# One layer of attention and routed low-rank feed-forward: low-rank products stacked into one fp32r product, the routing bias moved to GpSimd, the first norm moved whole to ScalarE, and a reordered prologue

## The reference, cut to what matters

```python
# x: (16, 256, 128) float32; two heads of 64
def layer(x):
    x = x + layernorm(attention(layernorm(x)))   # q, k, v, rotary on half of each head, softmax, Wo
    x = x + layernorm(ffn(layernorm(x)))
    return x

def ffn(x):                        # E = 4 experts of ranks 1, 2, 4, 8 (15 in all)
    base = x @ W.T
    proj = l2norm(x @ Wp.T + bp)   # 32 wide
    lw   = softmax(proj @ l2norm(sim) * exp(min(temp, CLAMP_MAX)))
    gate = where(arange(4) == argmax(lw), lw, 0)
    return base + sum_e gate[e] * (x @ Wd[e].T) @ Wu[e].T
```

## Time and profile before

| | |
|---|---|
| median of 3 executions | 150.28 us (150.28 to 150.42) |
| profiled execution | 150.36 us, of which the profiler's span is 148.6 us |
| granted TensorE clock, mean over the span | 0.966 |
| PE matmul | 132.5 us busy, 89% of the span |
| DVE | 129.8 us, 87% |
| ACT | 112.2 us, 76% |
| POOL | 87.3 us, 59% |

### The profile page before, as it was taken

One profiled execution on the slowest core, in us unless ns is written; L12 is line 12 of the kernel. 1 busy time (PEld: TensorE's weight loads), 2 busy tenths in 40 slices (PEclk: granted clock), 3 DMA queues, 4 the chain that ended last, 5 costly groups with the idle time before them and its releaser, 6 DMA issues.

```text
span 148.6 us, 3108 instructions
## 1 busy us (share of the span) xinstructions
PE 132.5 (89%) x883; PEld 107.0 (72%) x883; DVE 129.8 (87%) x574; ACT 112.2 (76%) x376; POOL 87.3 (59%) x148
## 2 busy tenths in 40 slices
PE   0989789999989999999999999999999998985470
PEld 0667567889878879887988798779878986963230
DVE  6878969989897999999999999789789898899933
ACT  3656395987978899789969996999699948664450
POOL 6320806641918595769576856788556964348552
PEclk9999999999999999999999999999999999999655
DMA  2633340000000000200020002000100010000013
GB/s 92 180 113 90 84 128 4 2 0 0 0 7 0 2 0 0 71 4 0 2 75 2 0 0 75 0 0 0 71 7 2 25 46 4 0 0 0 2 71 141
DMA packets 5266, 4.83 MB, mean 32 GB/s; under 512 B 594, under 2 KB 5250, under 8 KB 5250
## 3 DMA queue, kind: packets, MB, share of 16 engines
q1 hardware_dynamic: 5104, 4.51, 9.6%
q10 hardware_dynamic: 146, 0.13, 0.3%
HBM read 2.54 MB, written 2.10 MB: 31 GB/s over the span
## 4 chain that ended last, share of the span: by engine, by line
PE 71%; DVE 15%; ACT 5%; POOL 2%; issue 2%; DMA 2%; POOLq 1%; DVEq 0%; ACTq 0%
PE ps_s L1321 10%; PE ps_a L1341 9%; PE ps_z L1364 5%; PE ps_b L1341 4%; PE ps_a L1331 4%; PE ps_c L1341 4%; PE ps_b L1331 3%; PE ps_s L1352 2%; PE ps_c L1331 2%; PE ps_c L1310 2%; PE ps_z L1377 2%; PE ps_s L1310 2%; PE ps_d L1300 2%; PE ps_d L1298 2%; PE ps_d L1299 2%
## 5 line engine op out<-in xcount | busy, mean ns | idle before, releaser
L432 ACT ACTIVATE probs<-ps_s,neg_max 128x256 f32<-128x256 f32 x60 | 25.3, 488 | 9.7 <-DVE neg_max L669 9.6
L669 DVE TENSOR_REDUCE neg_max<-ps_s 128x2 f32<-128x512 f32 x30 | 20.3, 681 | 1.2 <-PE ps_s L1321 1.1
L1321 PE MATMUL ps_s<-qk_t 64*128 64x256 f32 x120 | 17.4, 409 | 0.0
L1341 PE MATMUL ps_a<-v_all,probs_t 128*128 128x129 f32 x120 | 16.5, 280 | 0.0
L1341 PEld LDWEIGHTS ps_a<-v_all,probs_t 128*128 128x128 f32 x120 | 14.6, 191 | 2.0 <-issue 2.0
L689 DVE SCALAR_TENSOR_TENSOR x_all<-y_all,rsy,x_all 128x128 f32<-128x128 f32 x32 | 14.0, 462 | 1.3 <-POOL rsy L294 0.7
L1321 PEld LDWEIGHTS ps_s<-qk_t 64*128 64x128 f32 x120 | 10.6, 191 | 5.0 <-issue 4.3
L279 POOL TENSOR_TENSOR turn<-qk,sin_x 128x256 f32<-128x256 f32 x15 | 11.0, 733 | 2.5 <-ACT qk L418 2.1
L282 POOL TENSOR_TENSOR qk<-qk,cos_x 128x256 f32<-128x256 f32 x15 | 11.7, 777 | 1.2
L290 POOL TENSOR_TENSOR inv_norm<-norm,power 128x4 f32<-128x4 f32 x7 | 7.2, 1027 | 8.3 <-DVE norm L738 8.3
L306 POOL TENSOR_TENSOR std<-ve,root 128x4 f32<-128x4 f32 x7 | 7.1, 1019 | 8.2 <-DVE ve L710 8.2
(11 more groups left out here) (336 smaller groups left out, 432.0 us busy)
## 6 DMA issues: line engine op xcount, KB each, us to landing
x_all<-x SPq DMA_DIRECT2D x7, 256.0 KB, 2.7
out<-x_all SPq DMA_DIRECT2D x7, 256.0 KB, 2.1
x_all<-x SPq DMA_DIRECT2D x2, 128.0 KB, 2.7
out<-x_all SPq DMA_DIRECT2D x2, 128.0 KB, 1.7
w_raw<-w_attn ACTq DMA_DIRECT2D x1, 128.0 KB, 2.7
w_raw<-w_attn SPq DMA_DIRECT2D x1, 128.0 KB, 3.0
bo_bp<-vectors SPq DMA_DIRECT2D x1, 80.0 KB, 3.3
ffn_raw<-w_ffn SPq DMA_DIRECT2D x1, 71.5 KB
```

The costliest lines, as they stand in the source:

```text
L432: last = act.activation(probs[:, u, j, :], scores_of(n, u)[:, j * T:(j + 1) * T], ACT.Exp, bias=neg_max[:, u, j:j + 1])
L669: dve.tensor_reduce(neg_max[:, u, :], scores_of(n, u)[:, :].rearrange("p (j k) -> p j k", j=TILES), AX.X, ALU.max, negate=True).then_inc(m ...
L1321: last = pe.matmul(scores_of(n, 2 * b + h)[:, j * T:(j + 1) * T], qk_t[r, b, 0, j * P:(j + 1) * P], qk_t[r, b, 1, :], start=True, stop=True)
L1341: last = pe.matmul(unit_of(n, u)[:, j * VW:(j + 1) * VW], probs_t[:, u, i, j * P:(j + 1) * P], v_all[:, at:at + VW], start=(i == 0), stop= ...
```

## The change

1. Low-rank term. `gated` and `gated_e` have 64 columns per tile: the fp32r rounding of the gates in lane 0, their remainder behind it, and the rounding again in lane 1. `wu_z` holds, per tile, the rounding of the up weights in one lane and their remainder in the next. So a transpose takes two tiles instead of four (two transposes for a group), and `low_rank` makes two fp32r products over all 128 rows. DVE makes the gates in two instructions, the remainder in a third one (`gates_low`), in the tail the same by halves.
2. On PE `turn_gated` stands behind `weigh(a, 0)` and `low_rank` behind `weigh(a, 1)`.
3. `scaled_bias` is a GpSimd instruction behind `deviation`, ahead of the second half of the rotary work.
4. `normalise` is on ACT for all four tiles; on ACT `qkt_copy(a + 1, 0)` stands ahead of `variance_y(a, 0)`.
5. Prologue: the first half's norm goes ahead of the rotary frequencies, the angles come after `first_low(0)`, statistics of group 1 are spread out, `qk_first(0)` goes ahead of the copy of the turned weights, and `rows_up(1)` ahead of both copies of v.

```diff
@@ gpsimd
+            def scaled_bias(n):
+                pool.wait_ge(std_ready, n + 1)
+                if n == 0:
+                    pool.wait_ge(post_dve, 5)
+                else:
+                    pool.wait_ge(route_ready, 2 * n)
+                pool.tensor_tensor(bias_s[:, :, :], bias_b[:, :].unsqueeze(1).to_broadcast([P, PT, RW]),
+                                   std2[:, :].unsqueeze(2).to_broadcast([P, PT, RW]), ALU.mult).then_inc(scaled, 1)
...
                     deviation(a - 1)
+                    scaled_bias(a - 1)
@@ scalar
             def normalise(n):
-                for t in (2, 3):
+                for t in range(PT):
...
-                if now:
-                    variance_y(a, 0)
                 if nxt:
                     qkt_copy(a + 1, 0)
+                if now:
+                    variance_y(a, 0)
@@ vector
-                dve.tensor_tensor(gated[:, :, 0:RANK], picked[:, :, :], rank_wide(total), ALU.mult).then_inc(gated_ready, 1)
+                dve.tensor_tensor(gate[:, :, :], picked[:, :, :], rank_wide(total), ALU.mult)
+                up = gated[:, :, :].rearrange("p t (s l) -> p t s l", s=2)[:, :, :, 0:RANK]
+                dve.tensor_tensor(up, picked[:, :, :].unsqueeze(2).to_broadcast([P, PT, 2, RANK]),
+                                  total[:, :].unsqueeze(2).unsqueeze(3).to_broadcast([P, PT, 2, RANK]), ALU.mult).then_inc(gate_up, 1)
+
+            def gates_low(n):
+                dve.wait_ge(gate_up, n + 1)
+                dve.tensor_tensor(gated[:, :, RANK:2 * RANK], gate[:, :, :], gated[:, :, 0:RANK].bitcast(F32), ALU.subtract).then_inc(gated_ready, 1)
...
-                if far:
-                    normalise(a + 2)
...
-                if last_:
-                    scaled_bias(a - 1)
@@ tensor
-                pe.transpose((ps_b if n >= LAST - 2 else ps_d)[:, 0:P], gated[:, :, :].rearrange("p t c -> p (t c)"), ident[:, :]).then_inc(dt_done, 1)
+                for k in range(2):
+                    last = pe.transpose((ps_b if n >= LAST - 2 else ps_d)[:, k * P:(k + 1) * P],
+                                        gated[:, 2 * k:2 * k + 2, :].rearrange("p t c -> p (t c)").bitcast(F32), ident[:, :])
+                last.then_inc(dt_done, 1)
...
-                    pe.matmul(z_of(n, k)[:, :, RW:ZW], gated_t[r, :], wu_z[r, 2 * k:2 * k + 2, :],
+                    pe.matmul(z_of(n, k)[:, :, RW:ZW], gated_t[:, k, :], wu_z[:, :, :],
...
+                if now:
+                    weigh(a, 0)
                 if done:
                     turn_gated(a - 2, (v_out, 4 * (a + 1) + 2) if nxt else (v_out, 4 * PAIRS) if now else (dt_out, a - 2))
                 if now:
-                    weigh(a, 0)
+                    weigh(a, 1)
                 if done:
                     low_rank(a - 2)
-                if now:
-                    weigh(a, 1)
```

More of the change, by code:

```diff
@@ L107, in layer @@
         picked = sb("picked", [P, PT, RANK])
-        gated, gated_t = sb("gated", [P, PT, LANE]), sb("gated_t", [P, P])
+        gate, gated, gated_t = sb("gate", [P, PT, RANK]), sb("gated", [P, PT, 2 * LANE], F32R), sb("gated_t", [P, 2, P], F32R)
         sq_z, var_z, rsz = sb("sq_z", [P, PT, E]), sb("var_z", [P, PT]), sb("rsz", [P, PT])
@@ L331, in end_factors_z, with first_factors @@
                 pool.tensor_tensor(rsz_e[:, half(k)], var_e[:, half(k)], power[:, half(k)], ALU.pow).then_inc(rstdz_e, 1)
+            def first_factors(k):
+                pool.wait_ge(var0, k + 1)
+                pool.tensor_tensor(rs1[:, 0, half(k)], ve1[:, 0, half(k)], power[:, half(k)], ALU.pow).then_inc(rstd0, 1)
+            first_factors(0)
             pool.wait_ge(base_ready, 1)
             pool.tensor_tensor(freq_c[:, 3:4], freq_c[:, 2:3], expo[:, :], ALU.pow).then_inc(inv_ready, 1)
-            for k in range(2):
-                pool.wait_ge(var0, k + 1)
-                pool.tensor_tensor(rs1[:, 0, half(k)], ve1[:, 0, half(k)], power[:, half(k)], ALU.pow).then_inc(rstd0, 1)
+            first_factors(1)
             pool.wait_ge(late_loaded, 32)
@@ L460, in gated_copy @@
                 act.wait_ge(dt_done, n + 1)
-                act.activation(gated_t[:, :], (ps_b if n >= LAST - 2 else ps_d)[:, 0:P], ACT.Copy).then_inc(dt_out, 1)
+                act.activation(gated_t[:, :, :].rearrange("p k c -> p (k c)"), (ps_b if n >= LAST - 2 else ps_d)[:, 0:2 * P], ACT.Copy).then_inc(dt_out, 1)
             def variance_z(n):
@@ L485, in end_gated_copy @@
                 act.wait_ge(dt_done_e, k + 1)
[L486 removed]
+                act.activation(gated_t_e[:, k, :], gated_bank[k][:, 0:P], ACT.Copy).then_inc(dt_out_e, 1)
             def end_variance_z(k):
@@ L526, in _ @@
                 if a == 0:
+                    rows_up(1)
                     v_first(0)
-                    rows_up(1)
                     v_first(1)
@@ L566, in _ @@
                     normalise(a + 2)
+                if nxt:
+                    qkt_copy(a + 1, 0)
                 if now:
                     variance_y(a, 0)
-                if nxt:
-                    qkt_copy(a + 1, 0)
                 if now:
@@ L653, in variance @@
                 dve.scalar_tensor_tensor(ve1[:, n % 2, :], tmp1[:, 1, :], 1.0 / E, tmp1[:, 2, :], ALU.mult, ALU.add).then_inc(var1, 1)
-            def normalise(n):
-                dve.wait_ge(rstd1, n - 1)
-                for t in (0, 1):
-                    dve.tensor_scalar(xn[:, t, :], x_all[:, rows(n, t)], rs1[:, n % 2, t:t + 1], nm1[:, n % 2, t:t + 1],
-                                      ALU.mult, ALU.add).then_inc(xn_ready, 1)
             def rows_low(n):
@@ L924, in later_weights @@
                     dve.wait_ge(post_mm, 2)
-                    for t in range(PT):
-                        rr = slice(LANE * t, LANE * (t + 1))
-                        last = dve.tensor_copy(wu_z[rr, t, :], ps_z0[rr, 0:E])
+                    link(dve.tensor_copy(wu_spare[:, :], ps_z0[:, 0:E]), post_link)
+                    for t in range(2):
+                        up, low = slice(2 * LANE * t, 2 * LANE * t + LANE), slice(2 * LANE * t + LANE, 2 * LANE * (t + 1))
+                        dve.tensor_copy(wu_z[up, t, :], wu_spare[up, :].bitcast(F32))
+                        last = dve.tensor_tensor(wu_z[low, t, :], ps_z0[low, 0:E], wu_spare[low, :].bitcast(F32), ALU.subtract)
                     last.then_inc(post_dve, 1)
@@ L1022, in _ @@
             dve.tensor_tensor(spatial, spatial, turn[:, 0, :, :, :].rearrange("p g h i -> p g (h i)"), ALU.add).then_inc(rope0_done, 1)
+            stats(1, 2)
             first_low(1)
-            for t in range(PT):
-                stats(1, t)
+            stats(1, 3)
             gap(1)
@@ L1038, in _ @@
             last.then_inc(shift1, 1)
-            dve.wait_ge(shift1, 1)
-            for t in (0, 1):
-                dve.tensor_scalar(xn[:, t, :], x_all[:, rows(1, t)], rs1[:, 1, t:t + 1], nm1[:, 1, t:t + 1],
-                                  ALU.mult, ALU.add).then_inc(xn_ready, 1)
+            later_weights(0)
             for a in PASSES:
@@ L1104, in _ @@
                     mean(a + 3)
+                if done:
+                    gates_low(a - 2)
+                if has(a + 3):
                     variance(a + 3)
```

69 lines of the change are left out of this document (40 added, 29 removed).

## The result

| | before | changed |
|---|---|---|
| median | 150.28 us | 153.64 us (153.57 to 153.68) |
| profiled execution, span | 150.36, 148.6 | 153.68, 151.9 |
| PE, DVE, ACT, POOL busy, share of the span | 89, 87, 76, 59% | 86, 83, 77, 60% |

The ratio is 1.0217, 95% interval 1.020 to 1.0234: 3.3 us slower, 1.1 us beyond the forecast of 152.5 and within its range.

What follows compares the result with a forecast made beforehand. PE was taken to bound the loop before the change. Profiled 150.36 + 3.0 (passes 2 to 5) + 0.2 (pass 6) - 1.0 (prologue) + 0 (tail) = 152.56, so 152.5 us; eight-in-ten range 149.5 to 154.0.

Steps and rivals of the forecast that it cites:

- So PE bounds the loop: Loop before the change: PE, busy 14.64 of 14.64 us in a middle pass, sets its length.
- PE stays the bound: Rival, passes: nothing waits for ACT, passes give 5 x -0.28, prologue -1.0, total 147.9 us; chance of a gain 0.17.
- The gates' copy at S+8.08: ACT, mid-pass: copy starts no sooner than 8.08 us after the pass's first scores (S); ACT idle 0.71 us.
- Four norm tiles ready at S+14.03, PE waits 0.9 at turn_x.: End of a pass: ACT's late norm makes PE wait 0.9 us at turn_x; pass 0.62 us longer, as a floor.
- The second lateness: ACT's copy of turned columns behind the next scores: row maximum slips about 0.57 us; 0.13 taken per pass.
- DVE is relieved and doesn't bound: DVE, passes: loses bias (0.52 us) and two norm tiles, gains two gate instructions of about 0.15 to 0.2.
- DVE and POOL hold each other: Rival, passes: POOL slower beside DVE, turn_x2 late too; 0.35 us more per pass, 153.9 us; chance 0.12.
- PE's saving: PE, passes 2 to 6: cheaper low-rank products, two transposes; work falls by 0.28 us per pass.
- The prologue: Before the loop: first exponentials at about 17.9, first projection near 20.6; -1.0 us, bounds +0.2 and -1.4.
- The bias on POOL: POOL, each pass: bias takes 0.73 us, with 0.52 as lower bound and about 1.0 by the skill; it fits.
- The tail: After the loop: faster low-rank products against more DVE instructions and waits; sum 0, bounds -0.5 and +0.5 us.
- Pass 1: Passes 0 and 1, larger norm but no gates: 0, bounds -0.3 and +0.4 us.

Runs made afterwards that it cites:

- e6: Kernel before, with only the stacked low-rank products (item 1 of the change): 150.11 us, ratio 0.9985.
- e2: Changed kernel, with turn_gated ahead of weigh 0 and low_rank ahead of weigh 1 on PE, as before the change: 152.64 us, ratio 1.015.
- e1: Changed kernel, with tiles 0 and 1 of the first norm on DVE again in the loop's passes: 151.15 us, ratio 1.005.
- e11: Kernel before, with only the first norm whole on ACT in the loop: 152.36 us, ratio 1.0125.
- e4: Changed kernel, with norm split, gates turned early and bias on DVE again, all three together: 149.50 us, ratio 0.9939.
- e13: e4, with DVE's gates ahead of the rotary products in passes 2 to 6, and weighted-sum work and a statistic between mean and variance: 147.42 us, ratio 0.9811.
- e5: Kernel before, with only the new prologue (item 5), including group 1's norm on ACT: 149.43 us, ratio 0.9936.
- e3: Changed kernel, with the scaled bias on DVE again: 153.12 us, ratio 1.0181.
- e9: e7, with the fourth row maximum on DVE between two residuals instead of behind both: 149.76 us, ratio 0.9963.
- e7: e4, with the mean of the statistics ahead of the gates on DVE instead of behind them: 150.69 us, ratio 1.0017.

## Why the prediction was right, and where its steps were not

**The outcome** (slower, in passes 2 to 5) came as forecast. The four passes were put at +3.0 and measured +3.25, pass 6 at +0.2 and measured +0.46, the prologue at -1.0 and measured -0.70, passes 0 and 1 at 0, where pass 1 gave -0.49, the tail at 0 and measured +0.78. The total is 1.1 above the forecast: 0.78 from the tail, and 0.32 as the sum of what the others missed in both directions. That a pass came near the forecast (0.82 against 0.75) is in part luck: the term of 0.62 at turn_x measured 0.13 at most, and two that had been put at 0.13 and at nothing measured 0.42 and 0.27.

**"So PE bounds the loop"** was too simple. The last residual before was handed to PE with nothing to spare, in passes 2, 3 and 4 alike. So a saving on PE alone was worth nothing there, and the rival "PE stays the bound" (147.9) could not have come from this change: e6 has PE's saving with the gates turned in the old place and the norm split, and its passes 2 to 4 are longer (14.90).

**The gates' copy at S+8.08, 0.71 of idle time ahead.** Measured S+8.17 and 0.52, released by PE: the step is right in place and time. But its worth isn't what the sum gave it. By e2 it costs nothing in passes 2 to 4, and 0.62 in each of passes 5 and 6.

**"Four norm tiles ready at S+14.03, PE waits 0.9 at turn_x."** ACT's norm was ready about when predicted (its last tile at S+14.18 against S+14.03, turn_x on PE at S+14.23 against a hand-over at S+14.08). PE's wait of 0.85 however lies nearly 3 us earlier, at turn_x2, and DVE ends it. This step failed: of two chains that end nearly together I had followed one. Between turn_x2 and the next scores the changed kernel takes 15.46 - 11.25 = 4.21 us against 14.64 - 10.56 = 4.08 before, so turn_x and what stands around it cost 0.13. Nor do these hang on the late gates: with the gates early again (e2) the stretch is still 4.21, with the norm split again (e1) 4.08, and with the norm alone (e11) 4.10.

**The second lateness** (copy of the turned columns behind the scores, row maximum later by 0.57, "0.13 more a pass") was the right mechanism and mis-sized. The first exponentials came 0.42 later and all 0.42 reached turn_x2, since DVE had nothing to spare there. e1 and e11 confirm it from both sides: the norm costs 0.56 in the changed kernel and 0.43 alone, the difference being the 0.13 behind turn_x2.

**"DVE is relieved and doesn't bound"** failed. Over the pass DVE works less (13.76 against 14.13), but between the first row maximum and the last residual it needs 72.05 - 62.91 = 9.14 us instead of 71.75 - 62.88 = 8.87, from the three gate instructions and what is held around them. These 0.27 are e6's 14.90 - 14.64, within 0.01. With 0.42 and 0.13 they make the 0.82 of a pass: 0.27 + 0.42 + 0.13. The rival "DVE and POOL hold each other", by which turn_x2 comes late as well, is thus true in its mechanism; its 153.9 us was 0.3 above the result.

**PE's saving** of 0.28 a pass was mis-sized and hidden. e4, e6 and e13 give 0.35 to 0.37 in passes 5 and 6, and passes 2 to 4 of e13 are 0.42 to 0.43 shorter than before. The new products take 0.32 a pass, not 0.24; what the forecast left out is that both weighings beside them are shorter too (last section).

**The prologue** by itself is worth 0.93 (e5), so -1.0 was right; in the changed kernel 0.2 of it is gone by pass 1. The forecast had the first exponentials at 17.9 (18.08 in e5, 18.62 in the changed kernel) and the first projection near 20.6 (20.96 in the changed kernel). Its rows:

```profile
16.55 1.65 ACT L426 ACTIVATE xn<-x_all,nm,rs 128x128 f32<-128x128 f32 x4 [0.31 <-DVE nm L1064]
17.28 0.71 DVE L939 COPY wu_raw<-ffn_raw 128x30 f32<-128x30 f32 x1
17.91 1.27 DVE L680 TENSOR_REDUCE neg_max<-ps_s 128x2 f32<-128x512 f32 x2
18.62 0.84 ACT L449 ACTIVATE probs<-ps_s,neg_max 128x256 f32<-128x256 f32 x2 [0.42 <-DVE neg_max L680]
```

The norm on ACT is as long as predicted; the row maximum stands behind the stack's second copy of the up weights, 0.71 for 30 columns, which e5 doesn't have; GpSimd's product had started 0.08 ahead of it, at 17.20. So the stack takes back part of what the prologue brings.

**The bias on POOL** took 0.60, between the two bounds. That it "fits" held in the passes (e3: no change). In the tail it cost 0.42, where PE waited for the rotary half behind it, an instruction that the prediction had named as queued there without pricing it.

**The tail.** The stack costs 0.34 there (e6), and with the bias that is 0.76 of the 0.78. The last two pairs of low-rank products, 1.22 and 1.06 long before, are two single products of 0.56 and 0.58, all at a granted clock of 0.50. That this saving didn't pay for six more instructions on DVE is argued; which of them stood on the path was not followed.

**Pass 1** (-0.49) was a term taken as 0 with bounds of -0.3 and +0.4. e6 has it, e5 does not: it comes from the stack; that it does so by shifting DVE's residuals against GpSimd's products fits the hold of 1.67 that became 1.08 in e6.

**Open:** why e9's timed executions are 0.7 below its profiled one, and 0.9 below e7's. Moving qkt_copy was not tried alone; e6, which lacks it, matches e4, which has it, within 0.02 in passes 2 to 6.

## What to carry to other kernels

Ask of each wait chain how much it has to spare at the instruction where it joins the bounding engine: here the engine with the lower busy share had none, and a gap of 0.06 us between its end and the other's start was the hand-over. Two small DVE instructions more, or two norm tiles on another engine ahead of a copy, went straight into each pass. And where DVE and GpSimd work side by side, put what reads PSUM, statistics and reductions beside GpSimd's long products, and other work on SBUF, two-input instructions above all, ahead of them or behind: the order alone (e4 to e13) was worth 2.1 us.
